# A two-block network on one Trainium2 core: a fourth weight buffer for the 64 experts, and contractions of 192 channels split 128 + 64 instead of 96 + 96

## The reference, cut to what matters

```python
h = tok(x)                                    # 768 -> 192 channels per patch
h = h + mamba_fwd_bwd(layernorm(h))           # two scans over the tokens
h = h + soft_moe(layernorm(h))                # 64 experts, one slot each per image
h = h + rwkv(layernorm(h))
h = h + attention_and_moe(layernorm(h))

# soft_moe: d, c = softmaxes of xn @ phi;  xs = d^T xn          (32 images x 64 experts x 192)
#   hid = gelu(xs @ w1[e] + b1[e])  192 -> 768;  ys = hid @ w2[e] + b2[e]  768 -> 192;  y = c ys
# rwkv: x1 = ln(x);  k, v, sr = x1 @ Wk.T, x1 @ Wv.T, sigmoid(x1 @ Wr.T)
#   x = x + (sr * bi_wkv(k, v)) @ Wo.T
#   x2 = ln(x);  kf = relu(x2 @ Wk_f.T) ** 2  (192 -> 768)
#   x = x + sigmoid(x2 @ Wr_f.T) * (kf @ Wv_f.T)
# attention_and_moe: q, k, v = ln(x) @ in_w.T + in_b;  softmax attention of 12 heads of 16
#   x = x + ctx @ out_w.T + out_b;  x = x + mlp(x);  x = x + sum of the top 2 of 4 experts on ln(x)
```

## Time and profile before

| what | value |
|---|---|
| median of 3 runs | 1512.79 us (1511.65 to 1516.04) |
| the profiled execution | 1509.02 us, of which the span is 1507.3 us |
| TensorE matmul busy | 1323.9 us, 88% of the span |
| VectorE, ScalarE, GpSimd busy | 915.8, 670.9, 554.6 us |
| mean granted TensorE clock | 0.952 |
| the chain that ended last | TensorE 54%, VectorE 20%, issue 10%, ScalarE 6%, DMA 5%, GpSimd 4% |

### The profile page before, as it was taken

One profiled execution on the slowest core, in us unless ns is written; L12 is line 12 of the kernel. 1 busy time (PEld: TensorE's weight loads), 2 busy tenths in 40 slices (PEclk: granted clock), 3 DMA queues, 4 the chain that ended last, 5 costly groups with the idle time before them and its releaser, 6 DMA issues.

```text
span 1507.3 us, 18440 instructions
## 1 busy us (share of the span) xinstructions
PE 1323.9 (88%) x6684; PEld 767.2 (51%) x6684; DVE 915.8 (61%) x1513; ACT 670.9 (45%) x1206; POOL 554.6 (37%) x399
## 2 busy tenths in 40 slices
PE   7979989898989867469988859979999999999998
PEld 6634445454545434244433445547856659445444
DVE  3789999999999999972100148855446624221022
ACT  4786767677777744042110117631552241313311
POOL 1478898988989887300000020012034302000000
PEclk9999999999999999769999969999999999999999
DMA  6405051422414040344999940000010001030101
GB/s 205 172 2 172 12 162 37 135 75 98 127 46 171 12 160 0 138 178 189 395 397 396 372 103 0 1 0 1 1 38 1 2 1 31 7 110 13 37 0 33
DMA packets 38773, 151.96 MB, mean 101 GB/s; under 512 B 10364, under 2 KB 14587, under 8 KB 33948
## 3 DMA queue, kind: packets, MB, share of 16 engines
q1 hardware_dynamic: 34588, 149.21, 27.6%
q10 hardware_dynamic: 4096, 1.58, 0.4%
HBM read 147.56 MB, written 1.63 MB: 99 GB/s over the span
## 4 chain that ended last, share of the span: by engine, by line
PE 54%; DVE 20%; issue 10%; ACT 6%; DMA 5%; POOL 4%; SPq 1%; ACTq 0%; DVEq 0%; POOLq 0%
PE ps L1876 52%; DVE arena L1474 7%; DVE arena L1463 5%; DMA arena<-in_e_b 4%; POOL arena L821 3%; ACT arena L923 2%; ACT ps L1034 1%; DVE stats L1371 1%; DVE arena L1759 1%; PE ps L1885 1%; ACT arena L928 1%; DVE arena L1483 1%; SPq L633 1%; DVE arena L1763 0%; DVE arena L1514 0%
## 5 line engine op out<-in xcount | busy, mean ns | idle before, releaser
L1876 PE MATMUL ps<-arena 128*32 128x192 f32 (+17 forms) x5236 | 946.4, 415 | 97.8 <-DVE arena L1524 22.2
L1876 PEld LDWEIGHTS ps<-arena 128*32 128x32 f32 (+15 forms) x5236 | 539.7, 154 | 475.7 <-issue 277.1
L821 POOL TENSOR_TENSOR arena<-arena 128x784 f32<-128x784 f32 x192 | 368.9, 1935 | 94.0 <-DVE arena L1474 93.4
L1876 PE MATMUL ps<-arena,ident 128*128 128x392 f32 x900 | 349.3, 517 | 48.3 <-POOL arena L821 40.0
L1474 DVE TENSOR_TENSOR_SCAN arena<-ps,arena 128x784 f32<-128x784 f32 x192 | 341.0, 1777 | 2.5 <-ACT ps L1034 2.5
L1876 PEld LDWEIGHTS ps<-arena,ident 128*128 128x128 f32 x900 | 169.6, 196 | 196.5 <-POOL arena L821 70.5
L1034 ACT ACTIVATE ps<-arena 128x384 f32<-128x384 f32 x384 | 207.9, 575 | 114.2 <-DVE arena L1474 113.4
L923 ACT ACTIVATE arena<-ps 128x392 f32<-128x392 f32 (+9 forms) x265 | 124.3, 487 | 294.7 <-PE ps L1876 206.2
L923 ACT ACTIVATE arena<-ps,arena 128x392 f32<-128x392 f32 (+2 forms) x191 | 103.4, 602 | 224.5 <-PE ps L1876 139.1
L1463 DVE TENSOR_TENSOR arena<-ps,arena 128x784 f32<-128x784 f32 x192 | 182.8, 953 | 8.0 <-ACT ps L1060 6.8
L1622 DVE COPY arena<-ps 128x384 f32<-128x384 f32 x32 | 16.3, 552 | 150.7 <-PE ps L2124 150.7
(11 more groups left out here) (201 smaller groups left out, 861.0 us busy)
## 6 DMA issues: line engine op xcount, KB each, us to landing
arena<-in_e_w SPq DMA_DIRECT2D x32, 2304.0 KB
arena<-bc_rows SPq DMA_DIRECT2D x128, 392.0 KB, 4.8
arena<-in_patches SPq DMA_DIRECT2D x4, 1176.0 KB, 7.5
arena<-comb_rows SPq DMA_DIRECT2D x1, 3136.0 KB, 10.7
arena<-in_mlp_w SPq DMA_DIRECT2D x5, 576.0 KB, 4.6
arena<-arena ACTq DMA_DIRECT2D x128, 12.0 KB, 8.6
arena<-in_mlp_w SPq DMA_DIRECT2D x5, 384.0 KB, 3.6
arena<-in_mlp_w SPq DMA_DIRECT2D x10, 192.0 KB, 4.0
```

The lines of the kernel that those rows point to most:

```text
L821: pool.tensor_tensor(pair(hbuf[:, at % SLOTS, :]), pair(hbuf[:, at % SLOTS, :]), c_all[:, n:n + 2, :], ALU.mult).then_inc(times_c, 1)
L1876: return pe.matmul(dst, lhsT, rhs, start=first, stop=last)
```

## The change

**Fourth buffer.** A fourth `w1e` buffer is placed over `xn`, `dlog` and `dbd`, which are dead once the slots `xs` are made (their order in memory changes for it). `first_layers(3)` is issued when the last `xs` product is made, and every later `first_layers(g)` when the hidden products of g - 4 are made. `second_layers` keeps its two buffers.

**128 and 64 rows.** `xaT` and `x5T` (96 partitions, two chunks) become `xaA`/`xaB` and `x5A`/`x5B`: 128 channels on all partitions, and the other 64 channels of two quarters above each other. The turns use `packed` instead of `transposed` (16 transposes of a half either way, of 128 columns instead of 96). `kvr_in`, `receptance`, `channel_hidden`, `queries_keys` and `value_rows` contract 128 rows and then 64. The number of matmuls is the same everywhere. In `channel_hidden` and `queries_keys` four outputs are made together: four products of 128 rows, then four of 64 rows with row halves taking turns. In `kvr_in`, `receptance` and `value_rows` each output, or pair of outputs, has its 128-row product and then its 64-row product.

**Biases.** The row of ones that added `in_b` inside the matmuls goes (and two memsets with it); the bias is added by ScalarE in `qk_out` and `ctx_t`, and `ctx_t` becomes two activations, one for each chunk of 96 channels. The weights for these products are stored on 128 partitions instead of 96, and the loads grow with them (`in_w` and `w_kvr` 432 KB to 576 KB, `w_kf` 576 KB to 768 KB, `w_rf` 144 KB to 192 KB).

```diff
@@ SyncE
             def first_layers(g):
-                b = g % 3
+                b = g % 4
...
             first_layers(2)
             second_layers(1)
-            for g in range(3, NG + 1):
+            s_xs.wait_filled(sp, 11)
+            first_layers(3)
+            for g in range(4, NG + 2):
                 if g < NG:
-                    s_h1.wait_filled(sp, 2 * (g - 3) + 1)
+                    s_h1.wait_filled(sp, 2 * (g - 4) + 1)
                     first_layers(g)
-                s_y2.wait_filled(sp, g - 3)
-                second_layers(g - 1)
+                s_y2.wait_filled(sp, g - 4)
+                second_layers(g - 2)
@@ TensorE, kvr_in
                     if j == 0:
-                        s_xaT.wait_taken(pe, 2 * q + 1)
-                        for c in range(2):
-                            ins = mm(bank(s_kvr.banks[i][0], 128, 0, QT), w_kvr[:, c, w * D:w * D + 128],
-                                     xaT[:, c, quarter(q)], c == 0, c == 1)
+                        h, k = divmod(q, 2)
+                        s_xaT.wait_taken(pe, 4 * h + 2 + k)
+                        dst, rows = bank(s_kvr.banks[i][0], 128, 0, QT), slice(64 * k, 64 * k + 64)
+                        mm(dst, w_kvr[:, 0, w * D:w * D + 128], xaA[:, quarter(q)], True, False)
+                        ins = mm(dst, w_kvr[rows, 1, w * D:w * D + 128], xaB[rows, h * QT:(h + 1) * QT], False, True)
...
+                        for h in range(2):
+                            mm(dst[h], w_kvr[:, 0, w * D + 128:w * D + D], xaA[:, quarter(2 * h + q)], True, False)
+                        for h in range(2):
+                            ins = mm(dst[h], w_kvr[rows, 1, w * D + 128:w * D + D],
+                                     xaB[rows, h * QT:(h + 1) * QT], False, True)
@@ TensorE, receptance
+                s_xbT.wait_taken(pe, 4 * k + 3)
+                for first in range(4 * k, 4 * k + 4, 2):
+                    both = [(n, 2 * pair_at(n) + j) for j in range(2) for n in (first, first + 1)]
...
+                    for n, tile in both:
...
+                        mm(dst, xaA[:, cols(tile)], w_rf[:, 0, :], True, False)
+                        ins = mm(dst, xaB[p0:p0 + 64, at:at + TILE], w_rf[p0:p0 + 64, 1, :], False, True)
...
-                    s_xbT.wait_taken(pe, 2 * (i // 2) + 1)
@@ TensorE, channel_hidden
+                for first in range(12 * k, 12 * k + 12, 4):
+                    for i in range(first, first + 4):
+                        _, m, j = WIDE[i]
+                        s_kf.fill(pe, i)
+                        mm(bank(s_kf.banks[i][0], 128, 0, QT), w_kf[:, 0, 128 * m:128 * m + 128],
+                           xaA[:, quarter(2 * k + j)], True, False)
+                    for i in range(first, first + 4):
+                        _, m, j = WIDE[i]
+                        rows = slice(64 * j, 64 * j + 64)
+                        mm(bank(s_kf.banks[i][0], 128, 0, QT), w_kf[rows, 1, 128 * m:128 * m + 128],
+                           xaB[rows, k * QT:(k + 1) * QT], False, True).then_inc(s_kf.filled, 1)
...
-                    pe.wait_ge(kf_ready, 6 * (i // 2) + 6)
+                    pe.wait_ge(kf_ready, 12 * k + 11 + i // 2 % 2)
@@ TensorE, queries_keys
-                    s_x5T.wait_taken(pe, 2 * q + 1)
...
+                for first in range(some.start, some.stop, 4):
+                    h = first // 8
+                    s_x5T.wait_taken(pe, 4 * h + 3)
+                    for i in range(first, first + 4):
+                        at, q = i % 8 // 2 * CH, 2 * h + i % 2
+                        s_qk.fill(pe, i)
+                        mm(bank(s_qk.banks[i][0], CH, 0, QT), in_w[:, 0, at:at + CH], x5A[:, quarter(q)], True, False)
+                    for i in range(first, first + 4):
+                        at, rows = i % 8 // 2 * CH, slice(64 * (i % 2), 64 * (i % 2) + 64)
+                        mm(bank(s_qk.banks[i][0], CH, 0, QT), in_w[rows, 1, at:at + CH],
+                           x5B[rows, h * QT:(h + 1) * QT], False, True).then_inc(s_qk.filled, 1)
@@ TensorE, value_rows
                 for j in range(2):
-                    at = (2 * i + j) * TILE
-                    for k in range(2):
-                        rows = CH + k
-                        ins = mm(bank(s_vb.banks[i][0], TILE, j * D, (j + 1) * D),
-                                 x5two[0:rows, k, at:at + TILE],
-                                 in_w[0:rows, k, 2 * D:3 * D], k == 0, k == 1)
+                    image = 2 * i + j
+                    p0 = 64 * (image // 8 % 2)
+                    at = (image // 16 * 8 + image % 8) * TILE
+                    dst = bank(s_vb.banks[i][0], TILE, j * D, (j + 1) * D)
+                    mm(dst, x5twoA[:, image * TILE:(image + 1) * TILE], in_w[:, 0, 2 * D:3 * D], True, False)
+                    ins = mm(dst, x5twoB[p0:p0 + 64, at:at + TILE], in_w[p0:p0 + 64, 1, 2 * D:3 * D], False, True)
@@ ScalarE, qk_out and ctx_t
-                    copy_out(s_qk, i, dst, bank(s_qk.banks[i][0], CH, 0, QT))
+                    copy_out(s_qk, i, (qT, kT)[n // 2][:, n % 2, quarter(q)], bank(s_qk.banks[i][0], CH, 0, QT),
+                             ACT.Identity, bias=in_b[:, n:n + 1])
...
-                copy_out(s_cx, i, ctxT[0:CH, :, cols(i)].rearrange("p c (j l) -> p c j l", j=2),
-                         v[:, :, :, 0:TOKENS])
+                s_cx.wait_filled(act, i)
+                for c in range(2):
+                    ins = act.activation(ctxT[0:CH, c, cols(i)].rearrange("p (j l) -> p j l", j=2),
+                                         v[:, c, :, 0:TOKENS], ACT.Identity, bias=in_b[:, 4 + c:5 + c])
+                ins.then_inc(s_cx.taken["act"], 1)
```

More of the change, by code:

```diff
@@ L54 @@
 RW_LOADS = 11
-TB_LOADS = 11
+TB_LOADS = 10
 MLP_LOADS = 6
@@ L1199, in turned_in @@
                 for i in some:
[L1200 to L1202 removed]
+                    rows, c = rows_of(i)
+                    copy_out(s, i, turned(i, xaA, xaB), turning(s, i),
+                             ACT.Identity, bias=aff[rows, row + 1, c:c + 1], scale=aff[rows, row, c:c + 1])
             def kvr_out(u):
@@ L2160, in _, with packed @@
                 ins.then_inc(s_mix.filled, 1)
+            def packed(s, src, ready, some=range(8)):
+                flat = src.rearrange("p t n -> p (t n)")
+                for i in some:
+                    h, c, k = i // 4, i // 2 % 2, i % 2
+                    s.fill(pe, i)
+                    for t in range(TQ):
+                        at = 8 * h + TQ * k + t
+                        ready(at + 1 if c == 1 and k == 0 else at)
+                        lo = at * D + (0 if c == 0 else 128 if k == 0 else 64)
+                        ins = pe.transpose(bank(s.banks[i][0], 128, t * TILE, (t + 1) * TILE),
+                                           flat[:, lo:lo + 128], ident[0:TILE, 0:TILE])
+                    ins.then_inc(s.filled, 1)
             def kvr_in(u):
```

172 lines of the change are left out of this document (78 added, 94 removed).

## The result

| | before | after |
|---|---|---|
| median | 1513.40 us (1511.65 to 1516.04, 4 runs) | 1569.65 us (1565.14 to 1577.68, 4 runs) |
| ratio, with its 95% interval | | 1.0376 (1.0328 to 1.0424) |
| the profiled execution, its span | 1509.02, 1507.3 us | 1572.04, 1570.3 us |
| mean granted TensorE clock | 0.952 | 0.918 |

The change makes the kernel 56 us slower. The direction was forecast, the size was not: 1569.65 us lies far outside 1514 to 1540.

The account below looks back on a forecast made before the run. It took DMA to bound the experts, TensorE rwkv, and TensorE, VectorE and ScalarE the attention loop. Terms -4.0 + 6.5 + 5.4 + 2.5 - 5.6 + 1.0 + 8.2 + 3.1 = +17.1 gave 1529.9 us, range 1514 to 1540.

Parts of the forecast that it names:

- The part on units: Prices for TensorE work: 0.163 us per 192-column MATMUL, 0.33 us per 392-column one, plus a price per row-count switch.
- third rival: Experts' stretch: the fourth buffer gives nothing, 1533.9 us, or some 1540 with the lower clock at more switches; chance 0.15.
- Fourth buffer, -4.0: Experts' stretch: weight stream one load shorter, last output call starting at 864.2 us; gain 4.0 us, bounds 0.7 to 8.6.
- kvr_in, +6.5: Keys and values products in rwkv: switches 4.8 and 1.4 us, one more written-back item 0.3 us, all on the chain.
- Receptance, +5.4: Receptance products of 16 token tiles: alternating 128 and 64 rows costs 16 x 0.34 us, with nothing covering it.
- waits, +2.5: Before receptance in each half: waiting for four written-back items instead of two costs 1.25 us twice.
- channel_hidden, -5.6: Hidden products: six groups of four outputs, each 4.35 instead of 5.28 us through side-by-side 64-row products.
- queries_keys, +1.0: Second half's queries and keys: longer wait +2.9 us, side-by-side products -1.9 us; first half covered.
- value_rows, 0.51 us a tile: Attention loop: three more switches a tile at 0.17 us each, counted for 16 tiles, +8.2 us.
- ctx_t, 0.26 us: Attention loop: one ScalarE activation becomes two, +0.26 us a turn for 12 turns, +3.1 us.
- The switch price: TensorE changing between 128 and 64 rows: 0.17 us at 98 weight columns, 0.20 at 128, 0.09 at 4.
- Rival 1: Switches cost nothing in the new places: 23.0 us less, so -5.9 us, 1506.9 us, faster; chance 0.08.

Follow-up runs that it names:

- e10_value_64: The changed kernel, with narrow products of kvr_in and receptance contracting all 128 rows, value_rows keeping 64: runs of 1521.54, 1521.67, 1565.30 and 1565.87 us.
- e3_narrow_128: The changed kernel, with the narrow products of kvr_in, receptance and value_rows contracting all 128 rows instead of 64: 1512.51 us, ratio 1.0001 to before.
- e1_buffer_only: The kernel before with the fourth buffer alone: 1510.58 us, ratio 0.998 to before.

## Why the prediction was wrong

**The step that failed** is the pricing of every edit at the full clock. The part on units took 0.163 and 0.33 us a MATMUL from stretches at the full clock, and the sum used them everywhere; a lower clock appears in it only as something at which a switch in `kvr_in` "may cost twice", and as "some 1540" in the third rival. That the edit itself could set the clock, by putting lone 64-row products between those of 128 rows, was in no term and no rival. It is worth some 36 of the 56 us, an estimate: e10_value_64 in the shorter of its two outcomes is 1521.6 us, and 11.6 us of switches for `kvr_in` and receptance (the sum's 4.8 + 1.4 + 5.4) would make 1533 for after at the clock of before, for which the sum of +17.1 was about right. That all of it comes from the 128 and 64 rows e3_narrow_128 shows, at 1512.51 us; whether few rows, the half-array mode or the switches do it in after stays open, as said above. The prediction saw the lower clock of the first `kvr_in` (0.82, 9.66 us for 24 matmuls) and took it as the price of a switch, not as a state that the edit could prolong.

Point by point:

- *Fourth buffer, -4.0*: right as far as can be told. -3.7 in e1_buffer_only, whose interval is -6.2 to 0.0 us; waits in front of output calls, as the last part said; the last output call at 863.84 us in e1_buffer_only and 861.97 in after, whose experts started 1.6 us early, where 864.2 was forecast.
- *kvr_in, +6.5*: the term is right for units 4 and 5, six outputs at 0.4 us (54.15 to 56.50 us is +2.35); the stretch of the units before them costs +13.2 us in place of some 4, 9.6 of it in the first 24 matmuls, all at the half clock (19.28 against 9.66 us). There e3_narrow_128 without the 64 rows stands at 42.79 us (934.98 - 892.19).
- *Receptance, +5.4, and waits, +2.5; channel_hidden, -5.6*: right where the clock held. The second half takes 21.05 us after 21.24, as the switches (+2.7) and the side-by-side products (-2.8) say. Its waits grew by 1.24 us (the earlier trace rows against the two rows below). The first half is at the half clock from 1023 to 1040 us and takes 52.49 us instead of 44.78.
- *queries_keys, +1.0*: the two stretches from the second half to the loop grew by 1.5 us together; right within what they can tell.
- *value_rows, 0.51 us a tile*: right to the digit (3.22 against 2.71), but counted 16 times where the chain passes it 12 times, as the text itself said for `ctx_t`. *ctx_t, 0.26 us*: 0.23. Together a turn of 6.74 us against "about 6.8". At the full clock the loop costs +8.7 us (90.69 - 81.96), where 11.3 were summed.
- *The switch price*, 0.17 to 0.20 us, is confirmed at the full clock by the weight loads below and by the loop. Rival 1 had no case.
- *Rival 3* (the buffer gives nothing) has the mean of e1_buffer_only and the traces against it, though its interval reaches 1.0. Its "lower clock at more switches" had the right object and the wrong size: a switch costs 0.25 to 0.30 us at the half clock, which on the 34 switches of `kvr_in` is some 3 us (34 x 0.1, an estimate) and not 36. What costs is that all of TensorE's work there takes twice as long.

ScalarE's write-back before the second receptance, after (chain):

```profile
1075.56 1.81 ACT arena L943 x3
...
1077.39 0.68 ACT arena L943
```

Weight loads in the second half's receptance and hidden products, after (timeline):

```profile
1078.61 0.24 PEld L1903 LDWEIGHTS ps<-arena 64*98 64x98 f32 x2 [0.25 <-issue]
...
1079.60 0.24 PEld L1903 LDWEIGHTS ps<-arena 64*98 64x98 f32 x2 [0.25 <-issue]
...
1090.39 2.27 PEld L1903 LDWEIGHTS ps<-arena 128*128 128x128 f32 x8 [0.56 <-issue]
...
1094.74 2.27 PEld L1903 LDWEIGHTS ps<-arena 128*128 128x128 f32 x8 [0.56 <-ACT arena L943]
```

The periods are 0.99 and 4.35 us, the two of the earlier trace rows.

## What to carry to other kernels

A row count is not free to choose at equal MATMUL time: before thinning a product on TensorE, look at the granted clock of its stretch, and add a case to the forecast in which all of TensorE's work there doubles. If the layout needs 64 rows and they don't run side by side, zero-padded weights on 128 rows held the clock here and took no longer. After a pause, look at how soon the full clock is back, and not only at whether it falls. When a kernel's runs come in two groups, tell both and not their median.

## What the runs showed of the hardware

- Rows at work can decide over the granted clock with all else alike: 128 + 72 rows 1516.06 us, 72 + 72 rows 1570.7 us, where TensorE's instructions are the same in number and length at the full clock.
- A busy TensorE may stay at 1.2 GHz. In after it is busy for 74.93 of 75 us from 1201 to 1276 us, with a granted clock of 0.50 throughout. The Trainium skill (TensorE: Matmul & The Clock Gate, Part 1: The HAM clock gate) ties the half clock to an idle and the full one to a busy engine. This trace agrees on the falls before `kvr_in` and the first receptance, which stand behind pauses of TensorE. It disagrees on the loop: the pauses of a turn there (0.65 and 0.15 us) are those of e3_narrow_128, whose clock holds, and unbroken work didn't bring the clock back.
- Once down, the loop stays down. Its last 64-row weights are loaded at 1252.89 us, but the half clock lasts until 1276 us, through 96-row products and transposes, and ends just before the last block's first products; at the half clock TensorE alone is the chain.
- Behind a pause, the first `kvr_in` had the full clock back after 3.4 us before (902 us; it starts at 898.62), after 5 us in e3_narrow_128 (897; 892.19) and after 23 us in after (by 918; 894.20).
- A switch between 128 and 64 rows costs 0.17 us at the full clock and 0.25 us at the half one with 98 weight columns (0.51 and 0.74 us for a turn's three), 0.20 and 0.30 us with 128. The Trainium skill (TensorEngine Tiling (Array Packing), Key Properties) says that a change of mode drains the array, which agrees, but has no price.
